# One block for both phases of a cross-attention and mixture-of-experts layer: w2 loaded and split during the last attention batches, expert rows turned by DMA, a new order on every engine

## The reference

```python
x = x + xattn(layernorm(x), mask, ctx, Wq, Wk, Wv, Wo, gate)
x = x + moe(layernorm(x), router_w, w1, w2)
# xattn: 32 heads of 16 columns; q, k, v from the normed x, with rotary positions on q and k
w = softmax(q @ k.T / 4 + mask);             o = w @ v
a = tanh(gate) * softmax(q @ (ctx @ Wk).T / 4);  o = o + a @ (ctx @ Wv)
return o @ Wo
# moe: the best 2 of 8 experts of each token, softmax over their 2 logits
y1 = rows_of_expert @ w1[e].T                # 512 -> 2 x 352
y2 = (silu(y1[:, :352]) * y1[:, 352:]) @ w2[e].T   # 352 -> 512
y[token] += weight * y2
```

## Time and profile before

| | before |
|---|---|
| median of 3 runs | 1605.39 us (1598.07 to 1605.72) |
| the profiled execution, and its span | 1610.79 us, 1609.0 us |
| mean granted clock of TensorE in it | 0.963 of full speed |
| busy: TensorE, VectorE, ScalarE, POOL | 1437.7 us (89%), 1017.6 us (63%), 1013.2 us (63%), 829.3 us (52%) |
| read from HBM, written | 69.61 MB, 35.72 MB |

### The profile page before, as it was taken

How to read it: one execution, slowest core, us unless ns; L and a number is a source line. 1 busy time by engine, 2 the same in 40 slices (tenths; PEclk the granted TensorE clock), 3 DMA queues, 4 the chain that set the end, 5 groups by cost and what they waited for, 6 DMA issues and landing times. The chain is left out here.

```text
span 1609.0 us, 46292 instructions
## 1 busy us (share of the span) xinstructions
PE 1437.7 (89%) x16909; PEld 844.2 (52%) x16910; DVE 1017.6 (63%) x2595; ACT 1013.2 (63%) x1332; POOL 829.3 (52%) x991
## 2 busy tenths in 40 slices
PE   3899779999999999999999999861699999999996
PEld 1355445555555555555555555530366666666663
DVE  5557768888888888888888888744433332333332
ACT  4578657878878887887887888741444344344342
POOL 5445645566566566556656655421344544444443
PEclk9999979999999999999999999985799999999998
DMA  5466868677777778768767786533354454454543
GB/s 188 99 122 131 99 98 129 134 145 129 131 138 135 134 130 150 132 127 151 127 141 132 144 134 113 100 77 82 111 85 87 79 87 82 80 89 79 84 86 52
DMA packets 368118, 183.19 MB, mean 114 GB/s; under 512 B 323216, under 2 KB 327312, under 8 KB 367440
## 3 DMA queue, kind: packets, MB, share of 16 engines
q1 hardware_dynamic: 349808, 143.59, 48.2%
q0 software_dynamic: 18144, 37.31, 13.4%
HBM read 69.61 MB, written 35.72 MB: 65 GB/s over the span
## 5 line engine op out<-in xcount | busy, mean ns | idle before, releaser
L779 DVE TENSOR_REDUCE mx<-md 128x8 f32<-128x1024 f32 x256 | 312.9, 1222 | 106.6 <-PE md L1062 100.3
L638 ACT ACTIVATE pr<-st 128x1024 f32<-128x1024 f32 x256 | 262.0, 1023 | 172.2 <-PE st L1092 137.7
L1407 PE MATMUL y<-w1s,hgT 128*128 x1704 | 281.8, 316 | 3.3 <-ACT hgT L1321 3.3
L1407 PEld LDWEIGHTS y<-w1s,hgT 128*128 128x128 f16 x1704 | 165.1, 99 | 96.1 <-issue 3.7
L1107 PE MATMUL av<-pr,vv 128*17 128x128 f32 x4096 | 164.4, 279 | 28.5 <-ACT pr L638 28.3
L1321 ACT ACTIVATE hgT<-px 128x1024 f16<-128x1024 f16 x71 | 72.7, 1024 | 155.4 <-PE px L1397 155.4
L1426 PE MATMUL y<-w2s,yT 128*128 (+1 forms) x639 | 150.3, 379 | 0.9 <-DVE yT L1385 0.9
L503 POOL TENSOR_TENSOR part<-part,tg_r 128x128 f32<-128x128 f32 x128 | 58.3, 456 | 172.2 <-DVE part L815 168.3
L1107 PEld LDWEIGHTS av<-pr,vv 128*17 128x17 f32 x4096 | 90.9, 97 | 94.2 <-ACT pr L638 43.8
L607 ACT ACTIVATE md<-msk 128x1024 f32<-128x1024 f32 x128 | 131.0, 1023 | 10.0 <-DVE mx L779 10.0
L1384 DVE COPY yT<-py 128x256 f16<-128x256 f16 x142 | 40.4, 284 | 149.9 <-PE py L1416 149.9
(11 more groups left out here) (190 smaller groups left out, 2849.1 us busy)
## 6 DMA issues: line engine op xcount, KB each, us to landing
wst<-in_w SPq DMA_DIRECT2D x32, 352.0 KB, 4.0
xin<-in_x SPq DMA_DIRECT2D x32, 256.0 KB, 3.2
cin<-in_ctx SPq DMA_DIRECT2D x32, 256.0 KB
xres<-in_x SPq DMA_DIRECT2D x32, 256.0 KB, 3.0
h_pairs<-ohs SPq DMA_DIRECT2D x32, 256.0 KB, 2.3
out<-x SPq DMA_DIRECT2D x32, 256.0 KB
msk<-in_mask SPq DMA_DIRECT2D x32, 128.0 KB
lrow<-lists SPq DMA_DIRECT2D x71, 1.0 KB, 3.5
```

The costliest lines, as they stand in the source:

```text
L638: act.activation(pr[:, :, :, :], st[:, :, :, :], ACT.Exp).then_inc(p_ex.sem, 1)
L779: dve.tensor_reduce(mx[:, 2 * path:2 * path + 2, 4 * o:4 * o + 4], md[:, :, :, :], AX.X, ALU.max).then_inc(d_max.sem, 1)
L1407: i = pe.matmul(y1[s.par][j][:, 0:F], hgT[:, s.par, a, c, :], w, start=(n == 0), stop=(n == 11))
```

## The change

- Both phases are in one block: each engine runs its attention part and goes on to its expert part without a barrier. The first list read waits for the lists and the tables, the first gather for the stored pairs, the first add for the stored output.
- Attention buffers lie in one region `room`, in which w2's pairs (`w2s`) lie later; w2's loads have five places (`w_q`, `w_k`, `w_v`, and parts of `vv` and `qkk`). SP issues the loads in tasks of the last two batches, ScalarE and VectorE split in tasks of the last batch and, for experts 5 to 7, VectorE behind the tables.
- The attention result and the second norm have pair buffers of their own (`os`, `hs` instead of `ohs`). x is normed in place: `nat` is gone, and the load of x waits for the low half of the batch before.
- Expert rows are turned by one DMA transpose on SP, into four buffers `hgT` from four buffers `hg`. In SP's step for slot s stand the list read of slot s and the transpose of slot s-2. The adds follow five steps behind instead of three.
- Every engine's list in `step(i)` is in a new order; the router's PSUM bank is bank 1.

The diff, cut:

```diff
+    os = sb("os", [P, 2, D], F16)
+    hs = sb("hs", [P, 2, D], F16)
...
-    home = dict(q=0, k=1, ak=0, v=1, avp=0, o=0, router=0, places=1, mturn=1)
+    home = dict(q=0, k=1, ak=0, v=1, avp=0, o=0, router=1, places=1, mturn=1)
...
+    w2s, w2f = keep["w2s"], keep["w2f"] + [
+        vv[:, :, :, :, :].rearrange("p a b h v -> p (a b h v)")[:, 0:KF * D].rearrange("p (c n) -> p c n", n=D),
+        qkk[:, 2, :, :, :].rearrange("p s j n -> p (s j n)").bitcast(F32).rearrange("p (c n) -> p c n", n=D)]
+    w2_in, w2_hi, w2_lo = keep["w2_in"], keep["w2_hi"], keep["w2_lo"]
...
         def load_x(n):
             source = dram["x"](n)
-            sp.wait_ge(x_n.sem, x_n.at(n.shift(-1)))
+            sp.wait_ge(x_lo.sem, x_lo.at(n.shift(-1)))
...
         def load_residual(n):
             source = dram["x"](n)
             sp.wait_ge(x_2.sem, x_2.at(n.shift(-1)))
             sp.dma_start(xres[:, :], source).then_inc(xr_in.sem(n), 16)
+            if n.n == NB - 2:
+                load_w2(0)
...
         def store_out(n):
             sp.wait_ge(x_2.sem, x_2.at(n))
             sp.dma_start(dram["out"](n), x2[:, :]).then_inc(out_st.sem(n), 16)
+            if n.n == NB - 2:
+                load_w2(1)
+                load_w2(2)
+            if n.n == NB - 1:
+                for e in (5, 6, 7):
+                    load_w2(e)
...
         def turn_out(n):
-            if n.n == NB - 1:
-                load_first_w2(n)
             sp.wait_ge(o_lo.sem, o_lo.at(n))
             sp.wait_ge(o_p.sem, o_p.at(n.shift(-1)))
-            sp.dma_start_transpose(turned(oT), rows(ohs)).then_inc(o_T.sem, 16)
+            sp.dma_start_transpose(turned(oT), rows(os)).then_inc(o_T.sem, 16)
+            if n.n == NB - 1:
+                load_w2(3)
+                load_w2(4)
...
+        def load_w2(e):
+
+            room = w2f[e % len(w2f)]
+            used = ((q_p,), (k_p, ak_p), (v_p, av_p), (av_pe,), (t_pe,))
+            if e < len(w2f):
+                for event in used[e]:
+                    sp.wait_ge(event.sem, event.at(LAST))
+            else:
+                sp.wait_ge(w2_hi.sem, 2 * (e - len(w2f)) + 2)
+                sp.wait_ge(w2_lo.sem, 2 * (e - len(w2f)) + 2)
+            sp.dma_start(room[:, 0:2, :], dram["w2a"][e]).then_inc(w2_in[e % len(w2f)], 16)
+            sp.dma_start(room[0:96, 2, :], dram["w2b"][e]).then_inc(w2_in[e % len(w2f)], 16)
...
+            run(turn_x, i - 7)
+            run(store_out, i - 11)
+            run(next_x, i - 6)
+            run(turn_h, i - 11)
...
+        def w2_high(e):
+
+            free = ((q_p, k_p, ak_p, v_p, av_p), (q_lo, k_lo), (q_p, k_p, ak_p, v_back), (*q_T, *k_T), (*q_T, *k_T, *ak_T),
+                    (av_pe, t_seed), (t_pe,), (t_pe,))
+            for event in free[e]:
+                act.wait_ge(event.sem, event.at(LAST))
+            act.wait_ge(w2_in[e % len(w2f)], 32 * (e // len(w2f)) + 32)
+            room = w2f[e % len(w2f)]
+            act.activation(w2s[:, e, 0:2, 0, :], room[:, 0:2, :], ACT.Copy, scale=WS).then_inc(w2_hi.sem, 1)
+            act.activation(w2s[0:96, e, 2, 0, :], room[0:96, 2, :], ACT.Copy, scale=WS).then_inc(w2_hi.sem, 1)
...
         def out_hi(n):
             act.wait_ge(n_o.sem, n_o.at(n))
+            act.wait_ge(o_T.sem, o_T.at(n.shift(-1)))
+            act.activation(os[:, 0, :], on[:, :], ACT.Copy).then_inc(o_hi.sem, 1)
+            if n.n == NB - 1:
+                for e in (0, 1, 2):
+                    w2_high(e)
+
+        def h_high(n):
+            act.wait_ge(h_n.sem, h_n.at(n))
             act.wait_ge(h_T.sem, h_T.at(n.shift(-1)))
             act.wait_ge(h2_st.sem(n.shift(-1)), h2_st.at(n.shift(-1)))
-            act.activation(ohs[:, 0, :], on[:, :], ACT.Copy).then_inc(o_hi.sem, 1)
...
-            act.wait_ge(o_T.sem, o_T.at(n))
-            act.activation(ohs[:, 0, :], hn[:, :], ACT.Copy).then_inc(h_hi.sem, 1)
+            act.activation(hs[:, 0, :], hn[:, :], ACT.Copy).then_inc(h_hi.sem, 1)
...
+            if n.n == NB - 1:
+                for e in (5, 6, 7):
+                    w2_high(e)
...
-            dve.wait_ge(x_hi.sem, x_hi.at(n.shift(-1)))
-            dve.wait_ge(x_lo.sem, x_lo.at(n.shift(-1)))
-            dve.tensor_scalar(nat[:, :], xin[:, :], mv[:, 0, 0:1], mv[:, 0, 3:4], ALU.subtract,
+            dve.tensor_scalar(xin[:, :], xin[:, :], mv[:, 0, 0:1], mv[:, 0, 3:4], ALU.subtract,
...
+        def w2_low(e):
+
+            room = w2f[e % len(w2f)]
+            dve.wait_ge(w2_hi.sem, 2 * e + 2)
+            dve.scalar_tensor_tensor(out=w2s[:, e, 0:2, 1, :], in0=room[:, 0:2, :], scalar=WS,
+                                     in1=w2s[:, e, 0:2, 0, :], op0=ALU.mult, op1=ALU.subtract).then_inc(w2_lo.sem, 1)
+            dve.scalar_tensor_tensor(out=w2s[0:96, e, 2, 1, :], in0=room[0:96, 2, :], scalar=WS,
+                                     in1=w2s[0:96, e, 2, 0, :], op0=ALU.mult, op1=ALU.subtract).then_inc(w2_lo.sem, 1)
...
         def residual(n):
+            if n.n == NB - 1:
+                for e in (0, 1, 2):
+                    w2_low(e)
...
         def h_low(n):
             dve.wait_ge(h_hi.sem, h_hi.at(n))
-            dve.tensor_tensor(ohs[:, 1, :], hn[:, :], ohs[:, 0, :], ALU.subtract).then_inc(h_lo.sem, 1)
+            dve.tensor_tensor(hs[:, 1, :], hn[:, :], hs[:, 0, :], ALU.subtract).then_inc(h_lo.sem, 1)
+            if n.n == NB - 1:
+                w2_low(3)
+                w2_low(4)
...
+        for e in (5, 6, 7):
+            w2_low(e)
...
+    hg = wo.rearrange("p (k a n) -> p k a n", k=LB, a=2)
+    hgT = wq.rearrange("p (k a c n) -> p k a c n", k=LB, a=2, c=NC_)
+    yo = [wk.bitcast(F32)[:, k * D:(k + 1) * D] for k in range(LB)]
...
+        sp.wait_ge(keep["list_st"], keep["list_all"])
...
             sp.wait_ge(w_row.sem, w_row.at(s.shift(-LB)))
-            sp.wait_ge(g_in.sem(s), g_in.at(s.shift(-LB)))
+            if s.off >= 2:
+                sp.wait_ge(g_in.sem(s.shift(-2)), g_in.at(s.shift(-2)))
             sp.dma_start(lrow[:, s.off % LB, :], source).then_inc(l_in.sem(s), 16)
             if isinstance(s.n, int) and s.n == 2:
-                load_last_w2()
+                sp.wait_ge(w2_lo.sem, 2 * NE)
+            if s.off >= 2:
+                turn_rows(s.shift(-2))
+            if is_last:
+                for k in (-1, 0):
+                    sp.wait_ge(g_in.sem(s.shift(k)), g_in.at(s.shift(k)))
+                    sp.wait_ge(up_p.sem, up_p.at(s.shift(k - LB)))
+                    turn_rows(s.shift(k))
+
+        def turn_rows(s):
+
+            sp.dma_start_transpose(hgT[:, s.off % LB, :, :, :].rearrange("p a c n -> p (a c) n"),
+                                   hg[:, s.off % LB, :, :].rearrange("p a n -> p (a n)")).then_inc(g_T.sem(s), 16)
 
         walk(sp, step)
...
             pool.wait_ge(l_in.sem(s), l_in.at(s))
-            pool.wait_ge(g_tp.sem, g_tp.at(s.shift(-2)))
+            pool.wait_ge(g_T.sem(s), g_T.at(s.shift(-LB)))
...
         def step(s, is_first, is_last):
             gather(s)
-            if s.off >= 3:
-                add_rows(s.shift(-3))
+            if s.off >= 5:
+                add_rows(s.shift(-5))
             if is_last:
-                for k in (-2, -1, 0):
+                for k in (-4, -3, -2, -1, 0):
                     add_rows(s.shift(k))
...
+    def scalar(act):
+        act.wait_ge(w2_lo.sem, 2 * NE)
...
-            if not is_last:
-                rows_turned(s.shift(1))
...
             e = number(pe, exi, s, NE - 1)
             inner(s, 0, e)
             if not is_first:
                 turn_inner(d)
             inner(s, 1, e)
-            if not is_last:
-                turn_rows(s.shift(1))
             if is_first:
-                pe.wait_ge(w2_lo.sem, w2_lo.at(Batch(0, 0), 2 * NE))
-                pe.wait_ge(w2_hi.sem, w2_hi.at(Batch(0, 0), 2 * NE))
+                pe.wait_ge(w2_lo.sem, 2 * NE)
             else:
...
+        block = both.enter_context(nc.Block())
+
+        @block.sync
+        def _(sp):
+            attention[0](sp)
+            experts[0](sp)
```

More of the change, by code:

```diff
@@ L119, in attention_phase @@
     iot, slot, tiles, ends, ex, begin, valid, at, exi, ati = keep["slots"]
-    wts = keep["qkv"] + [sb("w_o", [P, NC_, 2, D], F16)]
+    wts = keep["weights"]
     wq, wk, wv, wo = wts
+    xcs = part([2, D], F16)
+    xT = part([2, NC_, P], F16)
+    cT = part([2, NC_, P], F16)
+    t1 = part([D], F32)
+    t2 = part([D], F32)
+    t3 = part([D], F32)
+    xin = part([D], F32)
+    cin = part([D], F32)
+    avT = part([4, P], F32)
+    qs = part([NH, 4, HD], F16)
+    ks = part([NH, 4, HD], F16)
+    aks = part([NH, 4, HD], F16)
+    pr = part([2, 4, P], F32)
+    msk = part([2, 2, P], F32)
+    qkk = part([3, 2 * RING, 4, P], F16)
     identf = sb("identf", [P, P], F32)[:, :]
@@ L247, in walk @@
     def walk(step):
-        for i in range(NB + 9):
+        for i in range(NB + 11):
             step(i)
@@ L339, in turn_h @@
             sp.wait_ge(r_p.sem, r_p.at(n.shift(-1)))
```

(54 more changed lines are left out.)

425 lines of the change are left out of this document (185 added, 240 removed).

## The result

| | before | changed |
|---|---|---|
| median | 1604.18 us (4 runs, 1598.07 to 1605.72) | 1623.22 us (4 runs, 1617.52 to 1629.85) |
| ratio, 95% interval | | 1.0124 [1.0096, 1.0152] |
| profiled execution, and its span | 1610.79 us, 1609.0 us | 1617.52 us, 1615.8 us |

The kernel became 1.2% slower; 1567 us were forecast. The profiled execution of before is slower than its four runs and that of the changed kernel is the fastest of its four, so the spans differ by 6.8 us where the medians differ by 19.

A forecast was written before the change was run, and what follows sets the result against it. TensorE was taken to pace both phases. From 1610.8 us profiled, expert phase -28, boundary -10.6, drain 0 and attention 0 gave 1572.2; less 5.4 for the profiled run's excess over the median, 1567 us, range 1538 to 1596.

The forecast's parts named there:

- Attention phase, forecast 0: Attention batches: same matmuls and same loop in a new order, so 0 us, with ends of -31 and +38.
- attention loses: Attention phase: one reduction late per batch, +38 us, eating what the rest gains, 1605 us; chance 0.07.
- close the gaps: Attention phase: the new order also closes TensorE's gaps, 1.0 us per batch, giving 1536 us; chance 0.14.
- likely case: Whole kernel: the forecast of 1567 us itself, own range 1553 to 1581 us; chance 0.60.
- Expert phase, forecast -28: Expert slots: DMA transposes replace TensorE's, slot 6.32 to 5.92 us, 70 x 0.40 = -28 us (bounds -31.5 and +34).
- the lower bound: Expert slots: the added DMA transposes cost the scatter-adds nothing, leaving a slot of 5.87 us and -31.5 us.
- the collision: Expert slots: scatter-add collides with each transpose, landing 4.9 + 1.2 us, slot 6.8, +34 us, kernel 1629 us; chance 0.07.
- old-slot rivals: Expert slots: adds landing 0.7 us later keep the slot at 6.3 us, no expert gain, kernel 1595 us; chance 0.10.
- a sign of being wrong: Expert phase: POOL's tiny operation waiting for the add's landing instead of ScalarE's `yo` would show the prediction wrong.
- Boundary, forecast -10.6 for the second slot: Between phases: second slot starts at 1138.3 instead of 1148.95, -10.6 us (-6.6 to -14.6, depending on POOL's operation).
- Drain, forecast 0: Last attention batch: two waits go, 6 us, but w2 loads ahead of `hT` and splits take it back; 0 (-6 to +6).

The follow-up runs named there:

- the last two runs: Kernel with `gap` as tensor_scalar, plus either the second weight as tensor_scalar (1562.98 us) or the last three experts' w2 loads moved behind the last hT (1561.59 us).

## Why the prediction was wrong

**Attention phase, forecast 0, measured +50.7 us: this step failed.** The order rows were read for what the instructions wait for by semaphore, and for what stands behind the router's copy. The rival "attention loses" priced a reduction that is late by its own length, 38 us. What happened is neither: a one-column operation, 0.16 us by itself, was put beside two long POOL operations and held for 2.9 us, which made a batch 2.1 us longer (33.15 against 31.04). The sum gave such an operation no price beyond its own length. The trace of before had the sign: a 128x16 operation of 1.20 us and a 128x2 CAST of 0.87 us, where others of that size took 0.2; they were not looked at. One instruction in another form brings the last batch's q from 1047.43 to 984.87, ahead of the 996.70 of before. So the order itself costs nothing; nor does it close the gaps, as a rival had it: with the hold removed a batch takes 31.04 us. What that run is ahead comes from the first ten batches, in which executions differ by as much (q of batch 10 starts at 331.70 us there, at 338.43 and 336.91 in the last two runs, at 343.86 before and at 336.19 before with the one-input `gap`). With the hold removed the kernel takes 1559 us, in the 1553 to 1581 that the prediction gave its likely case.

**Expert phase, forecast -28: right.** Timeline of the changed kernel, the matmuls with w2 and SP and POOL between them:

```profile
1300.42 0.35 SPq L1313 DMA_DIRECT2D lrow<-lists  x1
...
1300.82 1.25 SPq L1326 DMA_TRANSPOSE w_q<-w_o  x1
1300.90 0.19 POOL L1355 TENSOR_TENSOR held<-held 128x1 f32<-128x1 f32 x1 [2.21 <-DMA out<-w_k,dst]
1300.92 2.12 PE L1451 MATMUL ma<-room,w_v 128*128 x9
...
1306.79 2.12 PE L1451 MATMUL ma<-room,w_v 128*128 x9
```

The slot is 5.87 us, the lower bound; TensorE waits for nothing. POOL's tiny operation now waits for the add before (1300.90), but the adds still land 4.9 us after issue and keep up. So the collision and the old-slot rivals are out, though the prediction had named that wait as a sign of being wrong. 70 x 0.45 = 31.5 us; the 32.5 of the table also hold what the second and third slot no longer wait for, less about 3 us at the end, where five adds instead of three are still to come (last product with w2 begun 17.9 us before the end instead of 15.1).

**Boundary, forecast -10.6 for the second slot, measured -14.5: right in its steps, but POOL's operation was priced too high.** The second slot begins at 1185.23, 18.0 us after the tables instead of 32.5, and from it on the kernel is 29.5 us shorter. In the changed kernel:

```profile
1167.03 0.23 DVE L1024 TENSOR_TENSOR wst<-wst 128x71 int32<-128x71 f32 x1
...
1170.10 0.81 POOL L1340 TENSOR_TENSOR held<-held 128x1 f32<-128x1 f32 x1 [6.91 <-issue]
...
1171.06 1.80 POOL L1341 DMA_INDIRECT w_o<-h_pairs,lrow  x1
...
1175.84 1.25 SPq L1326 DMA_TRANSPOSE w_q<-w_o  x1
...
1179.05 6.35 PE L1432 MATMUL md<-w1s,w_q 128*128 x24 [21.95 <-DMA w_q<-w_o]
```

The first expert matmul runs 11.8 us after the tables, not 15.1: POOL's tiny operation takes 0.81 us instead of the 3.98 of the earlier trace rows, so the gather goes out 3.8 us after the tables instead of 7.0. Transpose to matmul is 3.2 us, near the 3.0 of the earlier trace rows. The 3.98 us look like the hold seen above the other way round: in the trace of before, POOL's operation (1125.99 to 1129.97) runs beside VectorE's splits of w2 and ends with the last of them, at 1129.92.

```profile
1129.24 0.68 DVE L1361 SCALAR_TENSOR_TENSOR w2s<-w2f,w2s 96x512 f16<-96x512 f32 x1
```

**Drain, forecast 0: right in sum (+0.1), by parts that the runs bear out only in part.** The last `oT` still takes 5.7 us from its issue to TensorE (1133.49 to 1139.22), where the sum took the usual 3.0. The last hT takes 6.4 us (1148.55 to 1154.91) behind the loads of three experts, near the 6.9 counted (these are six loads, not three); but with those loads moved the drain is no shorter, and what TensorE and VectorE then wait for are `count`, which stands behind the splits, and the list entries. And the run with the attention phase of before shows that the stretch with the w2 tasks takes 14.8 us longer in the old order. Pair buffers of their own do not take that back: the run with the load of x moved has them, differs from the changed kernel only in the order of the tasks and the router's bank, and takes 134.1 us there. So the new order takes it back, which the prediction had not counted.

## What to carry to other kernels

Where a change moves instructions between two engines' orders, look for small VectorE operations with two SBUF inputs, and casts, that would fall beside long POOL operations: price them at the rest of POOL's run of operations. A group whose mean is several times that of others of its size is the sign, and is worth a look even where it costs nothing yet. What a hold cost here is how late the reductions behind it were for TensorE: one of 2.9 us ahead of a reduction cost 2.1 us per batch, two of 0.75 us, also ahead of reductions, 0.25 in all.

## What was not expected of the hardware

- VectorE's operation waited through two POOL operations that follow one another (1.28 and 2.13 us), not just for the end of the first.
- A one-column operation is held with two tensors as inputs (2.92 us in either form) and not with one tensor and a scalar per partition (0.21 us). One input alone is no safe sign: a 128x2 cast was held as well (`chosen_at`, 0.77 us in the changed kernel, 0.17 with the one-input `gap`).
- DMA transposes of 128x1024 beside gathers and scatter-adds, at 77% DMA load, did not delay the adds: 4.9 us to land, as before.
